# An expert mixture on one Trainium2 core: rows sorted without gaps, 39 visits of an expert to 32 blocks instead of 39 blocks, the opening in another order, and the second bias outside the products

## The reference, cut to what matters

```
scores = xf @ Wg
w, idx = jax.lax.top_k(scores, K)          # K = 2
w = jax.nn.softmax(w, axis=-1)
normed = xhat[None] * gamma[:, None] + beta[:, None]
h = jax.nn.relu(jnp.einsum('end,edf->enf', normed, W1) + b1[:, None, :])     # f = 512
out = jnp.einsum('enf,efd->end', h, W2) + b2[:, None, :] + xf[None, :, :]
y = jnp.einsum('ne,end->nd', cw, out)      # cw: w at the two chosen experts, else 0
```

## Time and profile before

| | |
|---|---|
| time, median of 3 executions | 1872.68 us (1869.92 to 1873.43) |
| the profiled execution | 1854.63 us, its span 1852.9 us |
| busy over the span | PE 92%, DVE 73%, ACT 51%, POOL 40% |
| TensorE's mean granted clock | 0.955 |

### The profile page before, as it was taken

One profiled execution on the slowest core, in us unless ns is written; L12 is line 12 of the kernel. 1 busy time (PEld: TensorE's weight loads), 2 busy tenths in 40 slices (PEclk: granted clock), 3 DMA queues, 4 the chain that ended last, 5 costly groups with the idle time before them and its releaser, 6 DMA issues. The chain is left out here.

```text
span 1852.9 us, 29706 instructions
## 1 busy us (share of the span) xinstructions
PE 1706.6 (92%) x10771; PEld 1267.7 (68%) x10771; DVE 1347.9 (73%) x2656; ACT 946.4 (51%) x1572; POOL 733.0 (40%) x617
## 2 busy tenths in 40 slices
PE   5988994799999999999899998898989999999897
PEld 4777883555655655555467776776668799867776
DVE  6976315677777777777588888798899854668698
ACT  3660554477777777777455554455000500155585
POOL 3640772355555555565413443564024011012231
PEclk9995997899999999999989999999999999999799
DMA  1004553000000000000002120000001100000032
GB/s 47 2 15 139 144 154 113 1 1 1 1 1 1 1 1 1 1 1 1 20 1 93 68 77 15 13 2 1 29 17 40 46 18 1 13 1 1 30 117 99
DMA packets 32940, 61.54 MB, mean 33 GB/s; under 512 B 5100, under 2 KB 18936, under 8 KB 30630
## 3 DMA queue, kind: packets, MB, share of 16 engines
q1 hardware_dynamic: 29846, 54.44, 9.0%
q0 software_dynamic: 2496, 5.12, 1.1%
q10 hardware_dynamic: 464, 0.20, 0.1%
HBM read 54.97 MB, written 4.78 MB: 32 GB/s over the span
## 5 line engine op out<-in xcount | busy, mean ns | idle before, releaser
L1975 POOL TENSOR_TENSOR sb_L_total<-sb_L_total,sb_L_probT 128x512 f32<-128x512 f32 x128 | 161.4, 1293 | 170.7 <-ACT sb_L_probT L2313 170.7
L446 POOL TENSOR_TENSOR sb_L_prob<-sb_L_prob,sb_L_rsum 128x616 f32<-128x616 f32 (+1 forms) x96 | 105.6, 1121 | 228.2 <-DVE sb_L_rsum L751 228.2
L2381 DVE TENSOR_REDUCE sb_L_tops<-banks 128x2 f32<-128x1024 f32 x128 | 156.4, 1223 | 22.9 <-PE banks L2089 21.7
L2313 ACT ACTIVATE sb_L_probT<-banks 128x1024 f32<-128x1024 f32 x128 | 124.8, 1025 | 74.0 <-PE banks L2123 73.5
L2136 PE MATMUL banks<-sb_L_probT,sb_L_v 128*64 128x512 f32 x512 | 129.0, 605 | 0.0
L2763 DVE SCALAR_TENSOR_TENSOR sb_L2f_hid<-banks,sb_L2f_weight,sb_L2f_hid 128x512 f32<-128x512 f32 x176 | 122.3, 745 | 3.1 <-PE banks L97 1.6
L1972 POOL TENSOR_TENSOR sb_L_total<-sb_L_probT 128x512 f32<-128x512 f32 x64 | 93.5, 1483 | 78.1 <-ACT sb_L_probT L2313 78.1
L2833 DVE SCALAR_TENSOR_TENSOR sb_resid<-banks,sb_L2f_weight,sb_resid 128x128 f32<-128x128 f32 x192 | 67.2, 351 | 62.4 <-PE banks L97 57.8
L1260 ACT ACTIVATE sb_L1f_gate<-banks 112x512 f32<-112x512 f32 x96 | 57.5, 599 | 92.5 <-PE banks L97 92.5
L534 PE MATMUL banks<-sb_ident,sb_L_prob 128*77 128x128 f32 x640 | 96.9, 284 | 4.2 <-POOL sb_L_prob L446 3.8
L648 ACT ACTIVATE sb_L_probT<-banks 77x512 f32<-77x512 f32 x160 | 87.1, 585 | 17.9 <-PE banks L534 17.5
(11 more groups left out here) (473 smaller groups left out, 4993.2 us busy)
## 6 DMA issues: line engine op xcount, KB each, us to landing
sb_L0f_hidden_w<-L0f_w SPq DMA_DIRECT2D x39, 256.0 KB
sb_L1f_wide<-spread_L1f SPq DMA_DIRECT2D x7, 1024.0 KB, 5.3
sb_L3f_wide<-spread_L3f SPq DMA_DIRECT2D x7, 1024.0 KB, 5.2
sb_fetched<-L2f_w SPq DMA_DIRECT2D x12, 256.0 KB, 2.6
sb_fetched<-L1f_gu SPq DMA_DIRECT2D x8, 336.0 KB, 3.2
sb_L0f_w<-L0f_w SPq DMA_DIRECT2D x1, 2072.0 KB, 7.9
sb_L0f_w<-L0f_w SPq DMA_DIRECT2D x1, 2048.0 KB
sb_L0f_returned<-L0f_results SPq DMA_DIRECT2D x8, 256.0 KB, 4.8
```

What stands on the lines that cost most here:

```text
L446: pool.tensor_tensor(grid, grid, bcast(rsum[:, n % PROBS, half], [None, KEYS]), ALU.mult).then_inc(normed, 1)
L1975: pool.tensor_tensor(sums, sums, probT[:, k, h], ALU.add).then_inc(added[h], 1)
L2313: act.activation(probT[:, k], ps[:, slot:slot + 2, :], ACT.Exp).then_inc(exped, 1)
L2381: dve.tensor_reduce(tops[:, :, k, 0], ps[:, banks:banks + 2, :], AX.X, ALU.max).then_inc(bound_read, 1)
```

## The change

What it does:

- **Sorting without gaps.** The pairs stand one behind the other, so that 4096 pairs fill 32 blocks exactly. A block in which one expert ends and the next begins is visited by both: 32 blocks and up to 7 more visits make `VISITS` = 39. A visit computes all 128 rows of its block with its expert, and `theirs` (0 or 1 for each row) keeps those that are the expert's. The results are added into `summed`, which POOL clears beforehand.
- **Gather, turning and scatter** are once for each of the 32 blocks. ACT now takes the turned rows into `turned_rows` unscaled. For each visit DVE reads the block's number into a register (`value_load` in `scale_rows`), scales the rows (L1796), adds the result (`collect`, L1804), and, 7 visits behind (`LAG`), multiplies a finished block by its weight (`weigh`, L1809). `AHEAD` is 16.
- **The second bias** leaves the loop. DVE sums up each row's weights by expert, PE turns them once (L1597), and four products of 512 columns (`biases`, L1633) give the weighted bias of all rows, which DVE adds to the residual (L1833). `b2` is now a 1 MB tile, zero apart from its diagonal blocks.
- **The opening.** PE scores batches 0 and 1 before it turns batches 2 and 3; the one-hot matrices are written group by group; DVE has more to work out about visits (`edge`, `tell`).
- **The end.** Half of the loads back are issued by ACT (`take_back`).

The core of the diff:

```diff
 SLOT = P
-BLOCKS = (2 * BATCH * SEQ + 8 * (SLOT - 1)) // SLOT
 TOKENS = BATCH * SEQ
-REAL = 4 * TOKENS
+BLOCKS = 2 * TOKENS // SLOT
+VISITS = BLOCKS + 7
...
-    E, F, BUFS, OBUFS, WBUFS, AHEAD, TALL = 8, 4, 8, 4, 4, 6, BATCH * SEQ // SLOT
+    E, F, BUFS, OBUFS, WBUFS, AHEAD, LAG = 8, 4, 8, 4, 4, 16, VISITS - BLOCKS
...
+        def take_back(eng, k):
+            for i in range(OBUFS):
+                eng.wait_ge(sent[i], 16 * len(range(i, BLOCKS, OBUFS)))
+            for b in range(BATCH):
+                at = k * TOKENS + b * SEQ
+                eng.dma_start(returned[:, k, b * TPB:(b + 1) * TPB], slots.results[at:at + SEQ].rearrange("(t p) d -> p t d", p=P)).then_inc(back_in[b], 16)
...
+                take_back(sp, 0)
...
+                pool.memset(summed[:], 0.0).then_inc(cleared, 1)
...
+                    pool.indirect_dma_start(out=slots.results, out_offset=bass.IndirectOffsetOnAxis(ap=listed[:, j:j + 1], axis=0),
+                                            in_=summed[:, j, :], in_offset=None).then_inc(sent[j % OBUFS], 16)
...
+                fetch.wait(pe, "small")
+                score(0)
+                score(1)
                 norm.turn(pe, 2, 0)
                 norm.turn(pe, 3, 1)
-                fetch.wait(pe, "small")
-                for b in range(BATCH):
-                    score(b)
+                score(2)
+                score(3)
...
+                pe.wait_ge(weighed, 1)
+                pe.transpose(ps[:, SPARE_BANK, 0:P], weights[:].rearrange("p n e -> p (n e)"), c.ident[:]).then_inc(weights_turned, 1)
...
-                        pe.wait_ge(out_ready, j - 1)
-                    at = ps[:, YBANKS[j % 2], 0:P]
-                    pe.matmul(at, ones[0:1, :], b2[0:1, bass.ds(e, 1), :].rearrange("p e d -> p (e d)"), start=True, stop=False)
+                        pe.wait_ge(out_taken, j - 1)
                     for f in range(F):
...
+                def biases(b):
+                    if b >= 2:
+                        pe.wait_ge(bias_added, b - 1)
+                    pe.matmul(ps[:, BIASES[b % 2], :], weightsT[:], b2[:, b * TPB:(b + 1) * TPB].rearrange("p n d -> p (n d)"), start=True, stop=True).then_inc(bias_done, 1)
+
+                pe.wait_ge(w2_in, 32)
+                pe.wait_ge(weights_ready, 1)
+                biases(0)
+                biases(1)
                 turn_rows(0)
                 turn_rows(1)
...
+                    if j - 2 in ADDED[0:2]:
+                        biases(2 + ADDED.index(j - 2))
...
-                    act.activation(x[:, j % 2, :], ps[:, XBANKS[j % 2], 0:SLOT], ACT.Copy, scale=fact[:, j, F:F + 1]).then_inc(x_ready, 1)
+                    act.activation(turned_rows[:, j, :], ps[:, XBANKS[j % 2], 0:SLOT], ACT.Copy).then_inc(x_taken, 1)
...
+                step(dve.tensor_tensor(weighted[:], top.hit[:], bcast(soft.exps[:], [None, E, None]), ALU.mult))
+                dve.tensor_reduce(weights[:], weighted[:], AX.X, ALU.add).then_inc(weighed, 1)
 
                 dve.wait_ge(ranked, 1)
-                step(dve.tensor_tensor(filled[:], bcast(ps[:, RANKS, P:P + E], [None, TALL]), bcast(limit[:], [E, None]), ALU.is_gt))
-                step(dve.tensor_reduce(blocks_of[:], filled[:], AX.X, ALU.add))
-                step(dve.tensor_tensor(shifted[:], lower[:], bcast(blocks_of[:], [E, None]), ALU.mult))
+                step(dve.tensor_copy(held[:], ps[:, RANKS, P:P + E]))
+                step(dve.tensor_tensor(shifted[:], lower[:], bcast(held[:], [E, None]), ALU.mult))
                 step(dve.tensor_reduce(begin[:], shifted[:], AX.X, ALU.add))
...
                 for n in range(0, TILES, GROUP):
-                    dve.tensor_tensor(at_place[:, n:n + GROUP], bcast(place_no, [GROUP, 2, None]), bcast(part[:, 1, n:n + GROUP], [None, None, SLOT]),
+                    at = slice(n, n + GROUP)
+                    step(dve.tensor_tensor(in_block[:, at], bcast(block_no, [GROUP, 2, None]), bcast(part[:, 0, at], [None, None, BLOCKS]), ALU.is_equal))
+                    dve.tensor_tensor(where[:, at, :, 0], in_block[:, at], bcast(named[:, at], [None, None, BLOCKS]), ALU.mult)
+                    dve.tensor_tensor(where[:, at, :, 1], in_block[:, at], bcast(soft.exps[:, at], [None, None, BLOCKS]), ALU.mult)
+                    dve.tensor_tensor(at_place[:, at], bcast(place_no, [GROUP, 2, None]), bcast(part[:, 1, at], [None, None, SLOT]),
                                       ALU.is_equal).then_inc(located, 1)
...
+                dve.tensor_copy(edge[:, 0], begin[:])
+                step(dve.tensor_tensor(facts[:, LAST, :], begin[:], held[:], ALU.add))
+                step(dve.tensor_scalar(edge[:, 1], facts[:, LAST, :], 1.0, 0.0, ALU.subtract, ALU.max))
...
+                def tell(first, last):
+                    at = slice(first, last)
+                    step(dve.tensor_tensor(facts_all[:, at], bcast(mine[:, at], [None, FACTS, None]), bcast(facts[:], [last - first, None, None]), ALU.mult))
+                    step(dve.tensor_reduce(fact[:, at], facts_all[:, at], AX.X, ALU.add))
+                    step(dve.tensor_tensor(visited[:, at], fact[:, at, OFFSET], visit_no[:, at], ALU.add))
+                    step(dve.tensor_scalar(standing[:, at], visited[:, at], float(SLOT), token_no[:, 0:1], ALU.mult, ALU.add))
+                    dve.tensor_tensor(inside[:, at], standing[:, at], fact[:, at, FIRST], ALU.is_ge)
+                    step(dve.tensor_tensor(theirs[:, at], standing[:, at], fact[:, at, LAST], ALU.is_lt))
+
+                    dve.tensor_tensor(theirs[:, at], theirs[:, at], inside[:, at], ALU.mult)
+                    step(dve.tensor_scalar(visited[:, at], visited[:, at], float(BLOCKS - 1), None, ALU.min))
+                    dve.tensor_copy(visited_no[:, at], visited[:, at]).then_inc(fact_ready, 1)
+
+                def scale_rows(j):
+                    q = dve.value_load(visited_no[0:1, j:j + 1], min_val=0, max_val=BLOCKS - 1)
+                    dve.wait_ge(x_taken, min(j, BLOCKS - 1) + 1)
+                    if j >= 2:
+                        dve.wait_ge(hid_done, (j - 1) * F)
+                    dve.tensor_scalar(x[:, j % 2, :], turned_rows[:, bass.ds(q, 1), :].rearrange("p q s -> p (q s)"), fact[:, j, F:F + 1], None, ALU.mult).then_inc(x_ready, 1)
+                    return q
+
+                def collect(j, q):
+                    dve.wait_ge(out_done, j + 1)
+                    if j > 0:
+                        dve.wait_ge(out_taken, j)
+                    sums = summed[:, bass.ds(q, 1), :].rearrange("p q d -> p (q d)")
+                    dve.scalar_tensor_tensor(out=sums, in0=ps[:, YBANKS[j % 2], 0:P], scalar=theirs[:, j:j + 1], in1=sums, op0=ALU.mult, op1=ALU.add).then_inc(out_taken, 1)
+
+                def weigh(b):
+
+                    dve.wait_ge(out_taken, b + LAG + 1)
+                    dve.tensor_scalar(summed[:, b, :], summed[:, b, :], share[:, b:b + 1], None, ALU.mult).then_inc(out_ready, 1)
+
+                tell(0, EARLY)
+                dve.wait_ge(fact_ready, 1)
+                visit = [scale_rows(0), scale_rows(1)]
+                tell(EARLY, VISITS)
+                dve.wait_ge(fact_ready, 2)
                 step(dve.tensor_reduce(total[:], soft.exps[:], AX.X, ALU.add))
                 step(dve.tensor_tensor(total[:], total[:], norm.inverse[:, 0, :], ALU.mult))
-
-                for j in range(BLOCKS):
+                dve.wait_ge(cleared, 1)
+
+                for j in range(VISITS):
+                    if j + 2 < VISITS:
+                        visit.append(scale_rows(j + 2))
                     if j < TILES:
                         step(dve.tensor_scalar(own[:], c.resid[:, j, :], norm.mean[:, j:j + 1], total[:, j:j + 1], ALU.subtract, ALU.mult))
                         step(dve.tensor_tensor(c.resid[:, j, :], c.resid[:, j, :], own[:], ALU.add))
-                    dve.wait_ge(out_done, j + 1)
-                    if j >= OBUFS:
-                        dve.wait_ge(sent[j % OBUFS], 16 * (j // OBUFS))
-                    dve.tensor_scalar(out[:, j % OBUFS], ps[:, YBANKS[j % 2], 0:P], share[:, j:j + 1], None, ALU.mult).then_inc(out_ready, 1)
+                    collect(j, visit[j])
+                    if j >= LAG:
+                        weigh(j - LAG)
+                    if j in ADDED:
+                        b = ADDED.index(j)
+                        dve.wait_ge(bias_done, b + 1)
+                        at = slice(b * TPB, (b + 1) * TPB)
+                        dve.tensor_tensor(c.resid[:, at], c.resid[:, at], ps[:, BIASES[b % 2], :].rearrange("p (n d) -> p n d", n=TPB), ALU.add).then_inc(bias_added, 1)
+                dve.wait_ge(bias_added, BATCH)
```

(6 more changed lines are left out.)

119 lines of the change are left out of this document (57 added, 62 removed).

## The result

| | time, us | span of its profiled execution, us |
|---|---|---|
| kernel before, runs shown ahead | 1872.68 (1869.92 to 1873.43) | 1852.9 (its time 1854.63) |
| changed kernel | 1854.54 (1854.15 to 1855.26) | 1852.8 (its time 1854.54) |
| forecast | 1854.5 (1847 to 1865) | 1834.7 (1852.9 less the sum of 18.2) |

The ratio is 0.9909 (95% 0.9891 to 0.9927): 0.7 to 1.1% faster, and the forecast is met to 0.1 us. The spans do not fit that. The profiled execution of before was 18 us faster than its runs, that of after was not faster than its own, and between the two profiles nothing was gained. What follows is about that.

What follows compares the result with a forecast made beforehand. PE was taken to bound the loop, POOL just behind. Last scatter 17.2 us earlier plus 1.0 for loads back, 18.2 off the profiled 1854.63, gives 1836.4; the runs' 18 above that execution makes it 1854.5 (1847 to 1865).

Steps and rivals of the forecast that it cites:

- The runs' median is 18 above that execution; with the same difference it becomes 1854.5.: Whole kernel: last step, carrying the runs' 18 us over the profiled execution from 1836.4 to 1854.5.
- visits of over 2.5 us and half clock for longer than one visit: Loop: two stated signs of a wrong prediction, DVE's visits over 2.5 us or TensorE at half clock beyond one visit.
- Opening: Before the loop: scores moved ahead of the turning and shorter DVE work bring the first hidden product 4.7 us earlier.
- Rival 5: Opening: POOL's clearing holds up DVE's normalisation and thus the turning, costing up to 2 us: 1856.5; chance 0.05.
- Start of the loop: First visits: DVE's second `tell` delays the third visit's scaling to 190.3 to 190.6; PE waits 2.3 us.
- The visits: Loop: 1.9 us for visits 0 to 6, 2.3 for 7 to 15, then 1.9, finally 1.78; four bias additions at 0.65.
- rival 1: Loop: a PE gap between hidden and result stays, 0.2 us in 31 visits, 6 us: 1861; chance 0.14.
- rival 2: Loop: the register load costs 0.3 us more on DVE, 6 us in all: 1860.5; chance 0.14.
- rival 3: Loop: register load so dear that DVE bounds every visit; at 1.2 us each, slower at 1884.6; chance 0.04.
- rule against it: Loop: the skill's floor of about 600 ns per `tensor_load` would make each DVE visit 0.3 us longer: 1860.5.
- Loads back: End: half the loads back move from one queue to ACT's, gaining 1.0 us (0 to 2).
- rival 4: Opening or loop start: part runs at 2.4 GHz as products fill pauses; gain 25 us, 1847.5; chance 0.1.

Runs made afterwards that it cites:

- ahead: Changed kernel with all 32 gathers ahead of the first scatter (AHEAD 32 for 16) and 20 buffers for 8: 1833.18 us, ratio 0.9911.
- plain: Changed kernel with GpSimd's 32 indirect gathers and 32 indirect scatters as ordinary DMAs of the same size: 1831.57 us, ratio 0.9755.
- best: `ahead` with the second `tell` in six pieces, residual steps at every second visit from 6 to 36, bias additions at 13, 21, 29, 37: 1827.26 us, ratio 0.9866.
- unit_back: Changed kernel with the bias as a product of one row in each visit again, without the four products and additions: 1866.13 us, ratio 0.9957.
- static: Changed kernel without register loads in the loop, expert and block written as constants on SyncE, TensorE and VectorE: 1850.54 us, ratio 0.9858.
- before_again: The kernel before, run again unchanged: 1875.88 us (1867.6 to 1878.94).

## Why the prediction was right, and where it wasn't

**"The runs' median is 18 above that execution; with the same difference it becomes 1854.5."** This step carried the number, and it had no reason behind it: that it held is luck. Both kernels lose the same where they are held up: 21.5 us between first and last scaling before, and 98.1 - 76.2 = 21.9 us in the summing after (the profile after against `ahead`). The loop that was measured is not the one forecast. Its last scatter starts at 293.1, not at about 271, visits took up to 5.2 us, and by the granted clocks above some 17 of the 78 us from 192 to 270 were at half speed; the prediction had named visits of over 2.5 us and half clock for longer than one visit as signs that it is wrong. Had the change made the kernel immune, as `plain` is, the time would have been 1832, far outside the range.

**The sum.** Forecast: last scatter 271.3, 18.2 less in all. `ahead`: last scatter 271.2, and a span of 1832.8, 20.1 under the profile of before; 17.3 of these lie ahead of the last scatter (288.5 to 271.2, forecast 17.2), the others behind the stage, where nothing was changed. Its parts were off and cancel:

*Opening, forecast 4.7, measured 2.6 to 3.0.* Rival 5 happened, and at more than its "up to 2". The timeline of after, and last the same instruction in the kernel before:

```profile
138.27 3.51 POOL L1548 MEMSET sb_L0f_summed<- 128x4096 f32 x1
138.37 3.43 DVE L251 TENSOR_SCALAR sb_norm_mean<-sb_norm_work 128x4 f32<-128x4 f32 x1
...
143.30 2.14 DVE L277 TENSOR_SCALAR sb_fetched<-sb_resid,sb_norm_mean,sb_norm_inverse 128x128 f32<-128x128 f32 x8
...
144.47 2.14 PE L287 MATMUL banks<-sb_ident,sb_fetched 128*128 128x128 f32 x8 [5.43 <-DVE sb_fetched L277]
...
164.88 13.76 PE L1602 MATMUL banks<-sb_L0f_where,sb_L0f_shared 128*128 128x64 f32 x64
...
178.68 0.19 DVE L1767 CAST sb_L0f_listed<-banks 128x32 int32<-128x32 f32 x1 [5.12 <-PE banks L1602]
...
184.48 1.82 PEld L1618 LDWEIGHTS banks<-sb_L0f_x,sb_L0f_hidden_w 128*128 128x128 f32 x8
```

```profile
138.71 0.17 DVE L251 TENSOR_SCALAR sb_norm_mean<-sb_norm_work 128x4 f32<-128x4 f32 x1
```

An operation of 4 numbers a partition ends with GpSimd's clearing, after 3.43 us (141.80; the clearing ends at 141.78). In the kernel before it took 0.17. The turning starts at 144.47 for 141.68, 2.8 later, which eats most of the 3.4 that the scores gave. "They have one input tile and are short" was the wrong argument: they are short, but the first of them waits for the whole clearing. The Trainium skill (SBUF — State Buffer, 🔬 SBUF: two separate sides) says that VectorE, in some forms of its operations, and GpSimd share a port pair, which the one that starts first holds for its whole instruction and shuts the other out. By that rule such an operation of VectorE waits for the clearing, and the trace agrees. No run moved the clearing, so the cause is read from this timeline alone. Behind it the account holds: the tables run as long as before, and they start 2.0 later than forecast (164.64, by their weight loads, for 162.6).

*Start of the loop, forecast: third scaling at 190.3 to 190.6, measured 192.71.* The second `tell` starts 1.7 later, for the opening, and its parts took 2.22, 2.22 and 1.4, as reckoned; 0.85 more passes before the scaling, for the register load and waits. `best` took this wait out.

*The visits, forecast 79.2 from the first summing to the last with one visit at half clock, measured 76.2 in `ahead`.* TensorE's 1.90 without gaps is right, as `unit_back` confirms from the other side (rival 1 falls). VectorE's visit with `weigh` was forecast at 2.3, and the bias additions at 0.65 each, 2.6 in all, more. The nine visits took 20.6 where the 2.3 alone make 20.7: the 2.6 didn't come. The visit with the addition at 206.66, say, took 208.28 - 206.39 = 1.89, so it lay in VectorE's slack. The clock of 0.96 from 192 to 230 (in `ahead` as in `plain`) is 3 us at half speed, an estimate from the mean, inside the one visit that was let in. The last visits, without a transposition, took 1.88 to 1.98, not 1.78.

*Register loads on VectorE.* 0.31 each in the median (0.30 to 0.55); with the visits above, rival 2 and rival 3 fall, and with them the 1860.5 of the "rule against it". `static` gained 5 by leaving them out on three engines.

*Loads back, forecast 1.0, measured none.* In the earlier trace rows the first issue is at 290.94 and the second batch's addition at 297.35, 6.4 later; in the profile after it is 295.43 and 302.13, 6.7. Two queues issue sooner (2.04 us for 5.50), but the first batch's addition starts 5.0 after the first issue, for 3.7 before:

```profile
294.62 0.69 DVE L1760 TENSOR_TENSOR sb_resid<-sb_resid,sb_L0f_returned 128x512 f32<-128x512 f32 x1 [6.38 <-DMA sb_L0f_returned<-L0f_results]
```

```profile
295.43 2.04 SPq L1517 DMA_DIRECT2D sb_L0f_shared<-L0f_results  x4
300.39 0.69 DVE L1839 TENSOR_TENSOR sb_resid<-sb_resid,sb_L0f_shared 128x512 f32<-128x512 f32 x1 [7.88 <-DMA sb_L0f_shared<-L0f_results]
302.13 0.69 DVE L1839 TENSOR_TENSOR sb_resid<-sb_resid,sb_L0f_shared 128x512 f32<-128x512 f32 x1 [0.32 <-DMA sb_L0f_shared<-L0f_results]
```

*The clock granted more (rival 4)* didn't happen where it counts: the tables took 13.76. From 187.5 to 191.0 it was granted 1.00 in the profile after, where the earlier trace rows have 0.51, but it had little to do there (1.57 us busy of 3.50) and waited for the third scaling; from 193 to 197 it was granted 0.66.

## What to carry to other kernels

A profile is one execution. Where it is 1% faster than the runs, find out what the runs lose before a sum is carried over to them; here it was luck that both kernels lose the same. A GpSimd instruction of several us that is "off the path" has a price if VectorE has something to do on the path at that time: put it where VectorE waits. And work that bounds nothing by its sum still costs where it stands in one piece ahead of something that is waited for: the second `tell`, cut up, gave the 4 us of the loop. The residual's steps, only moved to later visits, gave nothing in sum.

## What was not expected of the hardware

With indirect DMAs from GpSimd in the loop, VectorE waited up to 4.8 us for results of TensorE without a recorded release, ten times in before_again's loop of 117 us, VectorE of the changed kernel up to 3.6 us (5.7 in `static`), in two sets on two chips, and not at all in the sets at 1851 and 1854. Zeros as data, no weight loads, no register loads didn't remove it; ordinary DMAs of the same size did, in one run. Open are: whether the gather alone does it (the order in time points there; the two runs for it fell where nothing is held up), by what path it acts, why it comes and goes on a chip of one number, and whether `best` would be free of it in a set like the first two. The clearing was not moved in any run; by the timeline some 2.8 us are left there.
